# End of the last stage: two of every five tiles summed by TensorE with gates on diagonals, three by VectorE

## The reference, cut to what matters

```python
# x: (3125, 256) float32; 4 experts; w: (3125, 2) weights of the two chosen experts
out = jnp.zeros_like(x)
for ei in range(NUM_EXPERTS):
    g = jnp.where(topk_i == ei, w, 0.0).sum(-1)          # gate of each node for expert ei
    hh = jax.nn.gelu(x @ W1[ei] + b1[ei], approximate=False)
    out = out + g[..., None] * (hh @ W2[ei] + b2[ei])
...
x = x + out                                              # the result
```

## Time and profile before

| | us |
|---|---|
| median of 3 runs | 4336.94 (4331.12 to 4337.73) |
| the profiled execution, its own time | 4339.91 |
| its span in the trace | 4338.1 |
| VectorE busy over the span | 2983.7 (69%) |
| TensorE busy over the span | 3800.2 (88%) |
| ScalarE busy over the span | 2016.3 (46%) |

### The profile page before, as it was taken

The page is one execution under the profiler, slowest core; times in us unless marked ns, Lnnn a source line. Parts: engine busy times, 40 slices in busy tenths (PEclk is TensorE's granted clock), DMA queues, the critical chain, the costliest instruction groups (busy, mean ns, idle before and its releaser), DMA issues. The chain is left out here.

```text
span 4338.1 us, 87724 instructions
## 1 busy us (share of the span) xinstructions
PE 3800.2 (88%) x23737; PEld 3412.1 (79%) x23737; DVE 2983.7 (69%) x6878; ACT 2016.3 (46%) x4710; POOL 2146.7 (49%) x2102
## 2 busy tenths in 40 slices
PE   7899999999999997997999677777777599999993
PEld 6799999999999986997887666666666578888883
DVE  7799999999999987555333222333332389999997
ACT  3566666666666655776222000000000278888871
POOL 0455555555555530000000777777777177777781
PEclk9999999999999997998999556666665599999996
DMA  4566666666666640002444333333333223333225
GB/s 132 148 175 178 176 176 177 175 178 176 175 178 175 178 122 18 19 14 65 160 150 151 110 105 105 104 104 105 105 104 105 57 59 78 69 77 73 62 51 122
DMA packets 226996, 509.04 MB, mean 117 GB/s; under 512 B 51806, under 2 KB 94300, under 8 KB 220427
## 3 DMA queue, kind: packets, MB, share of 16 engines
q0 software_dynamic: 116736, 313.66, 26.1%
q1 hardware_dynamic: 106389, 187.30, 15.5%
q10 hardware_dynamic: 3679, 5.79, 0.4%
HBM read 434.08 MB, written 72.49 MB: 117 GB/s over the span
## 5 line engine op out<-in xcount | busy, mean ns | idle before, releaser
L685 POOL DMA_INDIRECT big<-table,e_idx x784 | 747.1, 953 | 887.6 <-DVE e_idx L721 649.1
L356 POOL DMA_INDIRECT big<-table,e_idx x784 | 767.3, 979 | 819.6 <-DVE e_idx L460 353.5
L703 PE MATMUL psum<-e_near_hot,big 128*128 128x64 f32 x3136 | 604.0, 373 | 279.2 <-issue 200.6
L703 PEld LDWEIGHTS psum<-e_near_hot,big 128*128 128x128 f32 x3136 | 581.5, 284 | 312.4 <-issue 237.6
L2190 POOL DMA_INDIRECT g_S<-gsrc,g_idx x512 | 614.2, 1200 | 194.5 <-issue 158.9
L468 DVE TENSOR_TENSOR big<-psum,big 128x512 f32<-128x512 f32 x784 | 539.1, 688 | 36.9 <-PE psum L375 26.5
L435 ACT ACTIVATE e_hT_hi<-psum 128x256 fp32r<-128x256 f32 x784 | 300.7, 384 | 552.7 <-PE psum L375 552.7
L748 DVE TENSOR_TENSOR big<-big,psum 128x128 f32 x196 | 56.5, 288 | 662.9 <-PE psum L703 546.3
L386 PE MATMUL psum<-e_w_hi,e_hT_hi 128*128 128x256 f32 x1568 | 507.0, 323 | 0.3 <-ACT psum L420 0.3
L386 PE MATMUL psum<-e_w_hi,e_hT_lo 128*128 128x256 f32 x1568 | 442.1, 282 | 0.0
L386 PE MATMUL psum<-e_w_lo,e_hT_hi 128*128 128x256 f32 x1568 | 438.8, 280 | 0.0
(11 more groups left out here) (395 smaller groups left out, 8942.5 us busy)
## 6 DMA issues: line engine op xcount, KB each, us to landing
big<-in_attr_t SPq DMA_DIRECT2D x392, 128.0 KB
g_rest<-gpart SPq DMA_DIRECT2D x128, 256.0 KB
big<-table,e_idx POOLq DMA_INDIRECT x1568, 2.8
table<-C SPq DMA_DIRECT2D x26, 896.0 KB
table<-n_rows SPq DMA_DIRECT2D x24, 896.0 KB
experts<-g_region SPq DMA_DIRECT2D x15, 560.0 KB
g_S<-gsrc,g_idx POOLq DMA_INDIRECT x512
table<-big SPq DMA_DIRECT2D x25, 224.0 KB
```

The costliest lines, as they stand in the source:

```text
L356: pool.indirect_dma_start(G[:, j % 2, q, :], None, table, bass.IndirectOffsetOnAxis(idx[:, j, q:q + 1], 0)).then_inc(s[f"G_in{j % 2}{q}"], 16)
L685: pool.indirect_dma_start(G[:, j % n, q, :], None, c.table1, bass.IndirectOffsetOnAxis(idx[:, j, q:q + 1], 0)).then_inc(s[f"G_in{j % n}"], 16)
L703: last = pe.matmul(acc[:, b, :], G[:, j % n, q, b * 128:(b + 1) * 128], onehot[:, q, :], start=q == 0 and (b == 0 or s is sems[1]), stop=q ...
```

## The change

In each group VectorE now does the first three tiles (`SUMMED` = 3), 60 instructions in place of 100; `added` starts at 3. The other two tiles of each group, ten in all (`product_tile(m)`, m from 0 to 9), are summed by TensorE in a PSUM bank: a matmul of the identity with the tile of X, and then for each expert a matmul whose stationary operand is a diagonal matrix 125 x 125 with the gates of that tile and that expert, and whose moving operand is the tile of the expert's rows. All are float32. ScalarE makes the diagonals: the identity, copied with the gate as scale of each partition. There are two sets of four diagonals, and set m % 2 is made again only after product m - 2 is done. ScalarE also copies each finished sum from PSUM back to its tile of X; four banks are used in turn. SyncE waits for VectorE's three tiles and for the group's two copies before it stores the group. The number and sizes of the stores stay as they were.

```diff
+    SUMMED, DIAG_AT = 3, 1100
...
+        gates_spread, gated, gated_kept = c.sem(tag + "gates_spread"), c.sem(tag + "gated"), c.sem(tag + "gated_kept")
+        BY_PE = GROUP - SUMMED
+        diag = rest[0:TP, DIAG_AT:DIAG_AT + 2 * E1 * TP].rearrange("p (j e n) -> p j e n", j=2, e=E1)
+
+        def gated_bank(m):
+            return c.ps[1 + m % 4][0:TP, 0:D]
+
+        def product_tile(m):
+            return m // BY_PE * GROUP + SUMMED + m % BY_PE
+
         with nc.Block() as block:
             @block.vector
             def _(dve):
-                dve.sem_inc(added, GROUP)
+                dve.sem_inc(added, SUMMED)
                 for g in range(NG):
                     for e in range(E1):
-                        for t in range(g * GROUP, (g + 1) * GROUP):
-                            i = (g * E1 + e) * GROUP + t % GROUP
-                            dve.wait_ge(added, i + 1)
+                        for q in range(SUMMED):
+                            t = g * GROUP + q
+                            dve.wait_ge(added, (g * E1 + e) * SUMMED + q + 1)
                             dve.scalar_tensor_tensor(out=c.X[:, t, :], in0=Y[e][:, t, :], scalar=c.gate[:, t, e:e + 1],
                                                      in1=c.X[:, t, :], op0=ALU.mult, op1=ALU.add).then_inc(added, 1)
+
+            @block.scalar
+            def _(act):
+                def keep(m):
+                    act.wait_ge(gated, m + 1)
+                    act.activation(c.X[:, product_tile(m), :], gated_bank(m), ACT.Copy).then_inc(gated_kept, 1)
+
+                for m in range(NG * BY_PE):
+                    if m >= 2:
+                        act.wait_ge(gated, m - 1)
+                    for e in range(E1):
+                        act.activation(diag[:, m % 2, e, :], c.ident[0:TP, 0:TP], ACT.Copy,
+                                       scale=c.gate[:, product_tile(m), e:e + 1]).then_inc(gates_spread, 1)
+                    if m:
+                        keep(m - 1)
+                keep(NG * BY_PE - 1)
+
+            @block.tensor
+            def _(pe):
+                for m in range(NG * BY_PE):
+                    t = product_tile(m)
+                    if m >= 4:
+                        pe.wait_ge(gated_kept, m - 3)
+                    pe.matmul(gated_bank(m), c.ident[0:TP, 0:TP], c.X[:, t, :], start=True, stop=False)
+                    for e in range(E1):
+                        pe.wait_ge(gates_spread, m * E1 + e + 1)
+                        last = pe.matmul(gated_bank(m), diag[:, m % 2, e, :], Y[e][:, t, :], start=False, stop=e == E1 - 1)
+                    last.then_inc(gated, 1)
 
             @block.sync
             def _(sp):
                 for g in range(NG):
-                    sp.wait_ge(added, (g + 1) * E1 * GROUP + GROUP)
+                    sp.wait_ge(added, (g + 1) * E1 * SUMMED + SUMMED)
+                    sp.wait_ge(gated_kept, (g + 1) * BY_PE)
                     for a, b in ROWS:
```

## The result

| | before | after |
|---|---|---|
| median, 6 runs each | 4337.33 us (4331.12 to 4341.37) | 4321.3 us (4312.87 to 4325.98) |
| the profiled execution, its own time | 4339.91 us | 4325.98 us |
| its span | 4338.1 us | 4324.2 us |
| from the end of the gates' write to the span's end | 44.6 us | 30.5 us |

The ratio is 0.9962, with a 95% interval of 0.9949 to 0.9974: 16.0 us by the medians, 13.9 us by the two spans. The last line of the table is the measure that the rest of this text goes by. It begins where L2909 (L2910 after) has ended its write of the gates and holds only the last block, so the scatter of the program before it (the whole times spread over 10 us before and 13 us after) is left out. I call it **the last stretch**.

What follows compares the result with a forecast made beforehand. VectorE's rate bounded the last block. Afterwards VectorE ends at 4317.97, TensorE at 4318.5 (4294.2 + 5.0 + 19.1 + 0.15), its copy at 4319.0: 14.8 us gained, median 4336.94 to 4322.1 us, range 4315 to 4333.

Steps and rivals of the forecast that it cites:

- VectorE's part: Last block: 40 of 100 instructions go at 0.396 us each, new wait free; VectorE ends 15.84 us earlier, at 4317.97.
- TensorE's prices: Ten new products, 100 matmul instructions: 0.427 us a step at the lower clock, 0.216 at the higher.
- The clock: TensorE's clock in the last block rises from 0.50 to 1.00 after 5.0 us, between 4.0 and 5.8 seen earlier.
- the sign: Expected trace evidence: new matmul instructions last 631 ns, then 379 after a clock rise 4 to 6 us in.
- ScalarE: Diagonals and PSUM copies: 0.29 us a step, 1.54 us per product, about 0.6 us ahead of TensorE; no table load.
- SyncE: Added wait before both stores of a group delays only later stores nobody reads; the tail of 4.3 us stays.
- The sum: End of the work moves from 4333.8 to 4319.0, 14.8 us earlier; profiled time 4325.1, median 4322.1 us.
- Rival 1: Identity and diagonal matmuls leave TensorE at the lower clock: 4340.7 us; chance 0.09, plus 0.03 with pauses on top.
- rows 8: Earlier trace stretch, 3428 to 3432: TensorE busy without pause, identity turns and 16-column matmuls, clock stayed at 0.50.
- Rival 2: TensorE not kept fed: diagonals at 0.49 us give 4323.6, 0.15 us gaps at waits 4328; chance 0.20 with rival 3.
- Rival 3: TensorE or ScalarE begins up to 2 us after VectorE: up to 4324 us; chance 0.20 together with rival 2.
- Rival 4: The groups' stores are the bound; excluded by 2.6 against 4.3 us unless transfers slow down, no chance given.

Runs made afterwards that it cites:

- the second: The changed kernel run again with nothing edited, against the kernel before: ratio 0.9948 (0.9932 to 0.9963), last stretch 29.1 us.
- the kernel with diagonals alone: Against the changed kernel: identity products made before the gates, three of seven banks a third time, twelve tiles on TensorE; last stretch 27.0 us, ratio 0.9964.

## Why the prediction was right, point by point

- **VectorE's part.** 60 instructions at 0.396: predicted end 23.84 us after its start, measured 23.85 (4294.35 to 4318.20). The wait that reaches back three places cost nothing.
- **TensorE's prices.** 0.427 and 0.216 us a step: the products at the higher clock take 2.16 us each, as worked out; at the lower one the first took 4.60.
- **The clock.** I took a rise after 5.0 us, from 4.0 and 5.8. It was 6.2 in the first profile and 3.2 in the second, both outside the 4 to 6 us that I had named as the sign; 5.4 with two and with four tiles for VectorE, and 5.9 with the diagonals made twice. The five have a mean of 5.2: right in the mean, and the spread is wider than the two rows showed. This term was under-sized by 1.2 us in the first profile, 0.6 us of time, which with 0.05 of the start gives TensorE's end at 4319.1 in place of 4318.5.
- **ScalarE.** Predicted step 0.29 and a period of 1.54 us with 0.6 to spare. Measured 0.29 (eight in 2.43 us, the last lasting 0.39) and 0.62 of idle time. No table was loaded.
- **SyncE.** I had costed the added wait at nothing, naming only who waits behind it. It costs about 0.3 us once, at the tail: this step was wrong, if small.
- **The sum.** 14.8 us predicted on the profiled execution, 13.9 measured. 0.2 of the difference lies ahead of the last stretch (gates written at 4293.72 in place of 4293.49). Within it 14.1: 0.6 less for the clock, 0.4 less for the tail, and 0.3 more since TensorE began 0.53 us after the gates, not 0.71, and the last handover and copy took 0.42, not 0.5. So errors of up to 0.6 us partly cancel. The median forecast was 4322.1 and is 4321.3; that they agree to 0.8 us is luck in part, as the six runs spread over 13 us and the interval of the ratio allows a gain of 11 to 22 us. What the traces confirm is the gain of the last stretch, 14.1 us, and how it is made up.
- **Rival 1**, TensorE stays cold, is refuted by both profiles of the change and by all the others: plain matmuls with the identity or a diagonal as stationary operand brought the clock up, and it stayed up wherever no long pause came between. (Its threshold of more than 82 steps follows with 0.7 us for what comes after the steps, as in its own time; with the 0.9 written there it is 81.) The Trainium skill's sentence on transposes, in "TensorE: Matmul & The Clock Gate", section "PE-mode transpose", doesn't extend to them: the granted clock in the kernel with diagonals alone was 1.00 for all of the 21 us. What held the clock down in rows 8 wasn't tried.
- **Rival 2** would have needed gaps at the waits. There were none in the change: ten instructions of a product in 2.16 us are ten steps of 0.216. Its other half, ScalarE as the bound, comes true only when ScalarE's work is doubled. **Rival 3**, a late start, didn't occur. **Rival 4**, the store as the bound, didn't come about in any of the kernels.

## What to carry to other kernels

When a bound engine's work can be split with an idle one, price both paths from rows of the trace at the clock that the idle engine will have, and put the cut where they end together; the rest of the gain then lies in what the second engine can do before the data that releases it is there. TensorE's low clock was a toll paid once per start, here 1.5 to 3 us; useful or empty matmuls in the wait before removed it, where the pause that they left was short (up to 2.8 us here; after 4.4 us the clock fell once more). A term whose position in time isn't fixed, like the rise of the clock, wants a spread from more than two rows.

## What was not expected of the hardware

- The same code had the clock rise 3.2 us after TensorE's start in one execution and 6.2 us in another, both after 16.35 us without a matmul.
- After a pause of 4.37 us TensorE began at 1.00 and fell to 0.50 0.8 us after it had begun again; after pauses of 1.03, 1.30, 2.60 and 2.76 us it didn't fall.
- A second wait, already satisfied, ahead of two stores lengthened their issue from 0.84 to 1.01 us; no run shows why.
